# Cross attention, first pass: three moved steps on VectorE and GpSimd, and one weight split moved to the stage's start

## The chip, the cores and the metric

One Trainium2 chip, one of its cores. The metric is the device time of one launch in microseconds (us), median of the runs shown. A profile is one further execution recorded by the hardware profiler. Engines: PE (TensorE), DVE (VectorE), ACT (ScalarE), POOL (GpSimd), SP (the DMA queue's engine).

## The reference, cut to what matters

The reference is a decoder of two layers; the change lies in the cross attention of layer 1, here in short (b over 8 batches, 128 positions each, width 256):

```
ln   = layernorm(x)
q, k, v, qx = fp8(ln / in_scale_m) @ w_m          # four matrices m, fp8: clamp, bf16, round to e4m3
kx, vx = split(ctx @ w_kv_x)
q, k, qx, kx = layernorm over each head of 128
core = softmax(q k^T) v        (16 heads, 8 key/value heads)
xout = softmax(qx kx^T) vx
x   += fp8(concat(core, xout) / proj_smooth) @ wproj * scales
```

The sixteen-bit matmuls on float32 weights need each weight split beforehand into a high and a low part: high = fp16(w * s), low = w * s - high.

## The kernel before, in words

Every engine has its own instruction list, written out by hand, and the engines meet only at semaphores; an instruction that waits holds all that stands behind it on its engine. The attention is worked through in 32 groups g (NG = 32): groups 0 to 15 are the first pass (core), groups 16 to 31 the second (xout), and each batch b takes two groups of a pass, one for each half of the heads. Group g+1's projections are computed inside group g's iteration.

In an iteration, with the functions of `cross`:

- PE: `project` (L1982 first pass, L1974 for the second pass's keys and values), `score` (L1999) in two halves, `project_out` (L2028), `turn_p` (L2007), `mix` (L2015), `turn` (L1989). Ahead of the first projection of group 16 it waits for all weight splits (w.split at len(w.chunks) = 26).
- DVE: `biggest` twice (the maxima of the scores, L2121), `divide` (reciprocal L2128, product L2131) and `variance` of the next group (L2142) in turns, `normalise` three times (L2147), in odd groups `add_out` (L2173), `smoothed` twice (L2159), `clip` (L2166, then L1886 and L1887 of `fp8_vector`), and in some odd groups `quantise_x` of a later batch (L2114, L1886, L1887).
- ACT: `square` (L2270, L2275), `weigh` (the exponentials, L2299), `take_pT`, `take_v`, `take_x` in odd groups, `take_turned` (L2291), and in the even groups named in `later` one weight chunk by `split_scalar` (L1441, L1443).
- POOL: `root` three times for the next group (L2379 with the first, then the power L2383), `add_c` (L2368) and `round_c` (L2373), which round the clipped output of the group before to fp8 by an addition and a subtraction, `split_pool` (the low part, L1449) in the groups of `later`, `add_x` (L2357) in even groups and `round_x` (L2362, L2363) in odd ones, which do the same rounding for the input of a later batch.

The rounding of an input batch b passes from `take_x` (ACT) to `quantise_x` (DVE) to `add_x` (POOL) to `round_x` (POOL); `quantise_x(b)` also waits until `round_x(b-1)` is done. The rounding of the output passes from `clip` (DVE) to `add_c` and `round_c` (POOL, one iteration later).

There are 26 weight chunks of 1024 columns. Fifteen are split in the scan before (IN_LOOP), three behind it, one (chunk 18) at the start of the cross attention by `last_splits` and `last_low`, and chunks 19 to 25 in groups 2, 4, ... 14.

The order of POOL in the iteration, before:

```python
            if g + 1 < NG:
                root(g + 1, 0)
            if g:
                add_c(g - 1)
            if g + 1 < NG:
                root(g + 1, 1)
                root(g + 1, 2)
            if g:
                round_c(g - 1)
```

Of the kernel before, what the change touches and what calls it, by code (L numbers as in the profile page):

```python
# [13 lines left out]
B, S, D = 8, 128, 256  # L14
# [990 lines left out]
def scan(k):  # L1005
# [9 lines left out]
    c_rows = [A.take([N])]  # L1015
# [5 lines left out]
    unsplit = [A.take([k.proj.SPLIT]), k.XN[:, 0:k.proj.SPLIT // D, :].rearrange("p b d -> p (b d)")]  # L1021
# [163 lines left out]
        for i in range(w.IN_LOOP, w.IN_LOOP + 3):  # L1185
            w.split_scalar(act, i, (unsplit[0], c_rows[0])[i % 2])

    def last_splits(act):
        for i in range(w.IN_LOOP + 3, w.IN_LOOP + w.TAIL):
            w.split_scalar(act, i, (unsplit[0], c_rows[0])[i % 2])  # L1190

    k.last_splits = last_splits

    def tensor(pe):
        k.turn_tensor(pe, 3, 2)
# [77 lines left out]
        for i in range(w.IN_LOOP, w.IN_LOOP + 3):  # L1273
            w.split_pool(pool, i, (unsplit[0], c_rows[0])[i % 2])

    def last_low(pool):
        for i in range(w.IN_LOOP + 3, w.IN_LOOP + w.TAIL):
            w.split_pool(pool, i, (unsplit[0], c_rows[0])[i % 2])

    k.last_low = last_low  # L1280

# [3 lines left out]
class Projections:  # L1285
# [144 lines left out]
            last = pool.tensor_tensor(self.factor[:, c, :], self.factor[:, c, :], self.ranged[:, 0:4], ALU.mult)  # L1430
        last.then_inc(self.factors_ready, 1)

    IN_LOOP, TAIL = 15, 4

    def split_scalar(self, act, i, tmp, buffers=2):
        if i == 0:
# [358 lines left out]
def cross(k):  # L1795
# [299 lines left out]
    def vector(dve, link):  # L2095
# [101 lines left out]
        for g in range(NG):  # L2197
            nxt = g + 1 < NG
            biggest(g, 0)
            biggest(g, 1)  # L2200
            divide(g, 0)
            if nxt:
                variance(g + 1, 1)
            divide(g, 1)
            if nxt:
                variance(g + 1, 2)
            if g in beside:
                moe.scale(dve, beside.index(g))
            if g == 30:
                moe.take_comb(dve, 0, ps[:, 6, :])  # L2210
            if nxt:
                for j in range(3):
                    normalise(g + 1, j)
            if g % 2 == 1 and g > 2:
                add_out((g - 3) // 2)
                if g > 2 * B + 3 and g != 27:
                    stats_of((g - 3) // 2 - B - 1)
                if g == 25:
                    stats_of(3)
                    moe.var_vector(dve, 0)  # L2220
            smoothed(g, 0)
            smoothed(g, 1)
            clip(g)
            if g == 0:
                quantise_x(2)
            if g % 2 and (g + 5) // 2 < B:
                quantise_x((g + 5) // 2)
            if g == 24:
                moe.total_vector(dve, ps[:, 6, 0:moe.PIECES])
            if g == 25:  # L2230
                moe.normalise(dve, 0, 0)
            if g == 26:
                moe.take_logits(dve, link, 0, 0, ps[:, 6, :])
                moe.normalise(dve, 0, 1)
            if g == 27:
                moe.take_logits(dve, link, 0, 1, ps[:, 6, :])
            if g == 28:
                moe.route(dve, link, 0)
# [14 lines left out]
    def scalar(act, link):  # L2253
        k.norm_twice(act, 7, [0])

        def take_x(b):
            act.wait_ge(lnT_psum, b + 1)
            wait(act, xs_ready, b)
            for r, m in enumerate(ROW):
                for c in range(KC if b else 1):  # L2260
                    last = act.activation(xy[:, r, c * S:(c + 1) * S], ps[:, 6, c * P:(c + 1) * P], ACT.Identity,
                                          scale=x_w[:, c, m:m + 1], bias=x_b[:, c, m:m + 1])
            last.then_inc(xy_raw, 1)

        def square(g, j):
            act.wait_ge(proj_psum, 4 * g + j + 1)
            if j == 0:
                wait(act, rs_ready, 3 * (g - 1) + 1)
                for i in range(MAXB):
                    last = act.activation(sq_k[:, i, :], ps[:, j, i * HD:(i + 1) * HD], ACT.Square,  # L2270
                                          accum_out=var[:, j, i:i + 1])
                last.then_inc(sq_ready, 1)
            else:
                wait(act, var_done, 2 * (g - 1) + j)
                act.activation(sq[:, (j - 1) * MAXB:j * MAXB, 0:HD], ps[:, j, :].rearrange("p (h d) -> p h d", d=HD),  # L2275
                               ACT.Square).then_inc(sq_ready, 1)

        def take_v(g):
            act.wait_ge(proj_psum, 4 * g + 4)
            wait(act, mixed, 2 * (g - 1))  # L2280
            out = flat(val[g % 2])
            act.mul(out, ps[:, 3, :], vx_inv if place(g)[0] else v_inv).then_inc(v_ready, 1)

        def take_turned(g, j):
            act.wait_ge(turn_psum, 3 * g + j + 1)
            wait(act, scores, 2 * (g - 1))
            if j == 0:
                wt = norms[:, 6:8] if place(g)[0] else norms[:, 2:4]
            else:
                wt = norm_q[:, 2:4] if place(g)[0] else norm_q[:, 0:2]  # L2290
            act.activation(flat(turned[g % 2][:, MAXB * j:MAXB * j + MAXB, :]), ps[:, j, :], ACT.Identity,  # L2291
                           scale=wt[:, 0:1], bias=wt[:, 1:2]).then_inc(turn_ready, 1)

        def weigh(g, t):
            n = 2 * g + t
            act.wait_ge(mx_ready, n + 1)
            wait(act, rden_ready, n - 1)
            for i in range(MAXB):
                last = act.activation(ps[:, 4 + t, i * P:(i + 1) * P], ps[:, 4 + t, i * P:(i + 1) * P], ACT.Exp,  # L2299
                                      bias=mx[:, t, i:i + 1], accum_out=den[:, t, i:i + 1])  # L2300
            last.then_inc(probs, 1)

        def take_pT(g, t):
            n = 2 * g + t
            act.wait_ge(pT_psum, n + 1)
            wait(act, mixed, n - 1)
            act.copy(flat(pT[t]), ps[:, 4 + t, :]).then_inc(pT_ready, 1)  # L2307

        act.wait_ge(consts, 1)
        take_x(0)  # L2310
        k.last_splits(act)
        square(0, 0)
        k.norm_twice(act, 8, range(1, B))
        act.activation(k.warm[:, :], k.eps[:, 0:1], ACT.Exp)
        square(0, 1)
        square(0, 2)
        take_v(0)
        take_x(1)
        for j in range(3):
            take_turned(0, j)  # L2320
        for g in range(NG):
            nxt = g + 1 < NG
            if nxt:
                square(g + 1, 0)
            weigh(g, 0)
            if nxt:
                square(g + 1, 1)
            weigh(g, 1)
            if nxt:
                square(g + 1, 2)  # L2330
            take_pT(g, 0)
            if nxt:
                take_v(g + 1)
            if g in (26, 27):
                moe.take_turned(act, 0, g - 26, ps[:, 6, :])
            if g == 28:
                moe.exponential(act, 0)
            take_pT(g, 1)
            if g == 0:
                take_x(2)  # L2340
            if g % 2 and (g + 5) // 2 < B:
                take_x((g + 5) // 2)
            if g in later:
                w.split_scalar(act, w.IN_LOOP + w.TAIL + later.index(g), unsplit, 1)
            if g in squaring:
                moe.square_piece(act, squaring.index(g))
            if g in beside:
                moe.high_part(act, beside.index(g))
            if nxt:
                for j in range(3):  # L2350
                    take_turned(g + 1, j)

    def gpsimd(pool, link):
# [29 lines left out]
            pool.tensor_tensor(rs[:, j, :], var[:, j, :], minus_half[:, j, :], ALU.pow).then_inc(rs_ready, 1)  # L2383

        pool.wait_ge(xq_ready, 1)
        k.last_low(pool)
        pool.wait_ge(k.x_done, 4)
        pool.memset(moe.minus_half, -0.5)
        pool.memset(moe.one, 1.0)
        link(pool.memset(minus_half, -0.5))  # L2390
        pool.wait_ge(consts, 1)
        for j in range(3):
            root(0, j)
        for g in range(NG):
            if g == 0:
                add_x(1)
            if g + 1 < NG:
                root(g + 1, 0)
            if g:
                add_c(g - 1)  # L2400
            if g + 1 < NG:
                root(g + 1, 1)
                root(g + 1, 2)
            if g:
                round_c(g - 1)
            if g in later:
                pool.wait_ge(cy_ready, g + 1)
                w.split_pool(pool, w.IN_LOOP + w.TAIL + later.index(g), unsplit)
            if g % 2 == 0 and 0 < g and (g + 4) // 2 < B:
                add_x((g + 4) // 2)  # L2410
            if g == 0:
                round_x(1)
                add_x(2)
            if g % 2 and (g + 3) // 2 < B:
                round_x((g + 3) // 2)
            if g == 28:
                moe.total_pool(pool, link)
            if g == 25:
                moe.rstd_pool(pool, 0)
            if g in (26, 27):  # L2420
                moe.x_low(pool, 0, g - 26)
            if g in beside:
                moe.low_part(pool, beside.index(g))
# [325 lines left out]
```

## Time and profile before

| what | value |
|---|---|
| median of 3 runs | 1042.55 us (1041.51 to 1043.96) |
| the profiled execution, its own time | 1043.24 us |
| its span, first to last instruction | 1041.4 us |
| mean granted TensorE clock | 0.953 |
| busy share of the span | PE 86%, DVE 75%, ACT 64%, POOL 53% |
| cross attention, first maxima to the last | 407.8 to 803 us in the span |

All times in the rows are us from the start of the span; a timeline row gives start, length, engine, line, operation, output and inputs, and in brackets how long the engine had been idle and who released it.

### The profile page before, as it was taken

What the parts mean: (1) busy time and instruction counts of PE and PEld (TensorE: products, weight loads), DVE (VectorE), ACT (ScalarE), POOL (GpSimd) and SP (SyncE); (2) the same over time, 40 slices, a digit from 0 to 9 for tenths busy, and PEclk for the clock granted to TensorE, in tenths of its full rate; (3) what the DMA queues carried; (4) which work ended last, traced back from release to release, by engine and by line L of the source; (5) the groups of instructions that cost most, each with busy time, mean ns of one, the idle gap of its engine ahead of it and who ended that gap; (6) DMA issues with size and microseconds to landing.
All of it is one profiled execution on the core that took longest, in us unless ns stands there. A gap on an engine that the chain in (4) does not pass through costs nothing.

```text
span 1041.4 us, 16045 instructions
## 1 busy us (share of the span) xinstructions
PE 896.2 (86%) x5388; PEld 577.4 (55%) x5388; DVE 779.8 (75%) x1345; ACT 671.6 (64%) x1585; POOL 555.9 (53%) x422
## 2 busy tenths in 40 slices
PE   6898899567566657888889999999999998999998
PEld 3665543234122224666666767777777665556565
DVE  4578879887999987877777757778877766664454
ACT  2656479787766657988887867887766455433222
POOL 3312447261699964788888766677666443410000
PEclk9899899788799987999999999999999999999999
DMA  9832205001121100000000060230002421223221
GB/s 330 342 140 78 86 0 177 14 1 44 41 81 67 74 21 1 1 2 1 1 1 22 21 180 24 73 106 2 1 2 65 160 66 57 73 60 88 71 67 40
DMA packets 38725, 69.77 MB, mean 67 GB/s; under 512 B 5378, under 2 KB 25282, under 8 KB 37108
## 3 DMA queue, kind: packets, MB, share of 16 engines
q1 hardware_dynamic: 38644, 68.75, 20.0%
q8 instruction: 43, 0.70, 0.3%
q14 instruction: 38, 0.31, 0.1%
HBM read 67.56 MB, written 1.18 MB: 66 GB/s over the span
## 4 chain that ended last, share of the span: by engine, by line
PE 31%; DVE 24%; POOL 19%; issue 17%; ACT 6%; DMA 2%; SPq 0%; POOLq 0%; DVEq 0%; ACTq 0%
PE ps L2467 10%; DVE arena L1126 6%; PE ps L2496 5%; POOL arena L2383 5%; POOL arena L2368 5%; POOL arena L2373 4%; DVE ps L1122 4%; PE ps L451 2%; PE ps L491 1%; DMA wide<-in_w_down 1%; PE ps L727 1%; PE ps L729 1%; PE ps L728 1%; PE ps L484 1%; POOL arena L2357 1%
## 5 line engine op out<-in xcount | busy, mean ns | idle before, releaser
L2383 POOL TENSOR_TENSOR arena<-arena 128x4 f32<-128x4 f32 x96 | 99.1, 1034 | 47.2 <-DVE arena L2142 44.5
L2299 ACT ACTIVATE ps<-ps,arena 128x128 f32<-128x128 f32 x256 | 88.4, 354 | 33.6 <-DVE arena L2121 33.5
L2514 DVE TENSOR_TENSOR arena<-ps,arena 128x512 f32<-128x512 f32 (+1 forms) x56 | 38.7, 690 | 86.4 <-ACT ps L2507 86.4
L2467 PE MATMUL ps<-XT,wide 128*128 128x512 f16 (+1 forms) x384 | 92.4, 379 | 0.9 <-DVE arena L2533 0.9
L2507 ACT ACTIVATE ps<-ps,arena 128x512 f32<-128x512 f32 (+1 forms) x56 | 36.9, 659 | 82.1 <-PE ps L2467 82.1
L2291 ACT ACTIVATE arena<-ps,ones 128x512 f32<-128x512 f32 x96 | 68.3, 788 | 29.2 <-PE ps L1989 29.2
L2121 DVE TENSOR_REDUCE arena<-ps 128x4 f32<-128x512 f32 x64 | 43.5, 689 | 57.7 <-PE ps L1999 57.7
L1271 POOL TENSOR_TENSOR arena<-arena 128x1024 f32<-128x1024 f32 x31 | 72.9, 2354 | 21.1 <-DVE arena L1126 18.9
L2496 PE MATMUL ps<-wide,arena 128*128 128x256 f16 (+1 forms) x672 | 82.2, 272 | 0.1
L2496 PEld LDWEIGHTS ps<-wide,arena 128*128 128x128 f16 (+3 forms) x672 | 65.4, 98 | 19.9 <-issue 0.8
L1999 PEld LDWEIGHTS ps<-arena 128*128 128x128 f32 x512 | 68.6, 196 | 10.3 <-ACT arena L2291 1.2
L1126 DVE TENSOR_TENSOR_SCAN arena<-arena,ps 128x1024 f32<-128x1024 f32 x32 | 73.2, 2287 | 1.1
L1982 PE MATMUL ps<-wide,arena 128*128 128x512 f16 x256 | 66.3, 394 | 8.6 <-DVE arena L2108 5.5
L2028 PE MATMUL ps<-side,arena 128*128 128x256 f16 x512 | 71.9, 275 | 0.0
L2015 PE MATMUL ps<-arena 128*128 128x256 f32 x256 | 69.1, 395 | 0.9 <-ACT arena L2307 0.9
L1999 PE MATMUL ps<-arena 128*128 128x128 f32 x512 | 68.9, 279 | 0.7 <-ACT arena L2291 0.7
L2373 POOL TENSOR_TENSOR arena<-arena 128x1024 bf16<-128x1024 f32 x32 | 68.3, 2136 | 0.2
L2147 DVE TENSOR_TENSOR arena<-ps,arena 128x512 f32<-128x512 f32 x96 | 61.5, 683 | 7.5 <-POOL arena L2383 6.9
L1222 PE MATMUL ps<-arena,ident 128*128 128x512 f32 x128 | 61.7, 604 | 1.9 <-POOL arena L1271 1.6
L1179 ACT ACTIVATE arena<-arena 128x1016 f32<-128x1016 f32 x32 | 36.5, 1142 | 39.0 <-DVE arena L1126 39.0
L1405 POOL TENSOR_TENSOR wide<-wide,head_mean 128x1024 f32<-128x1024 f32 x12 | 22.7, 1896 | 71.0 <-DVE head_mean L1400 71.0
L2028 PEld LDWEIGHTS ps<-side,arena 128*128 128x128 bf16 x512 | 50.5, 99 | 16.1 <-issue 0.7
(341 smaller groups left out, 2371.1 us busy)
## 6 DMA issues: line engine op xcount, KB each, us to landing
arena<-scan_rows SPq DMA_DIRECT2D x16, 512.0 KB, 3.5
arena<-comb_rows SPq DMA_DIRECT2D x26, 256.0 KB, 3.2
side<-in_wproj SPq DMA_DIRECT2D x4, 1024.0 KB, 5.5
arena<-in_w_down SPq DMA_DIRECT2D x7, 512.0 KB, 3.8
wide<-in_w_down SPq DMA_DIRECT2D x1, 3584.0 KB, 15.9
side<-in_w_gate SPq DMA_DIRECT2D x1, 3520.0 KB, 19.4
side<-in_w_up SPq DMA_DIRECT2D x1, 3520.0 KB, 12.5
wide<-in_w_gate SPq DMA_DIRECT2D x2, 1728.0 KB, 12.2
```

The source lines that it names most:

```text
L1126: dve.tensor_tensor_scan(state[c], dA[c], product, 0.0, ALU.mult, ALU.add).then_inc(state_ready, 1)
L1271: pool.tensor_tensor(read[c], state[c], c_rows[n % 2], ALU.mult).then_inc((read0_ready, read1_ready)[c], 1)
L1982: last = pe.matmul(ps[:, bank, :], x[:, c * S:(c + 1) * S], rhs, start=(i == 0), stop=(i == len(steps) - 1))
L1999: last = pe.matmul(ps[:, 4 + t, i * P:(i + 1) * P], tt[:, MAXB + h, :], tt[:, h // 2, :], start=(i == 0), stop=True, skip_group_check=True)
L2015: last = pe.matmul(ps[:, 4 + t, 2 * i * P:(2 * i + 2) * P], val[g % 2][:, 2 * t + i, :], flat(pT[t][:, 2 * i:2 * i + 2, :]), start=(i == 0 ...
L2028: last = pe.matmul(ps[:, 7, 0:D], cq[g % 2][:, i, :], w.parts(k.side, ((2 * path + half) * QH + i) * D)[part][:, 0:D], start=(half == 0 an ...
L2291: act.activation(flat(turned[g % 2][:, MAXB * j:MAXB * j + MAXB, :]), ps[:, j, :], ACT.Identity, scale=wt[:, 0:1], bias=wt[:, 1:2]).then_i ...
L2299: last = act.activation(ps[:, 4 + t, i * P:(i + 1) * P], ps[:, 4 + t, i * P:(i + 1) * P], ACT.Exp, bias=mx[:, t, i:i + 1], accum_out=den[: ...
L2373: pool.tensor_tensor(flat(cq[g % 2]), flat(cs), flat(cm[g % 2]), ALU.subtract).then_inc(cq_ready, 1)
L2383: pool.tensor_tensor(rs[:, j, :], var[:, j, :], minus_half[:, j, :], ALU.pow).then_inc(rs_ready, 1)
L2467: last = pe.matmul(self.ps[0:m, 2 * up + n % 2, :], y[:, c, :], x[:, c, :], start=(t == 0), stop=(t == len(steps) - 1))
L2496: last = pe.matmul(self.out(b), x[0:m, b * S:(b + 1) * S], y[0:m, :], start=(j == 0 and b % 2 == 0 and t == 0), stop=(j == MC - 1 and t == 2),
```

## The change

Four edits, all in the cross attention.

1. DVE: `quantise_x` of batches 3 to 7 moves from the end of odd group g-1 to even group g, behind the two `biggest` and ahead of `divide`. Batches 1 and 2 stay where they were.
2. POOL: `round_x` in odd groups additionally waits for cy_ready, that is, for the end of `clip` of its own group.
3. POOL: in groups 1 to 15 `add_c` moves from between the first and the second `root` to behind the third.
4. One more chunk is split outside the loop: TAIL goes from 4 to 5. Chunk 19 is split at the start of the stage, by ACT behind chunk 18 into the spare buffer of the loop, by POOL between `root(0, 0)` and `root(0, 1)`. `later` shrinks to groups 2, 4, ... 12, and group 14 has no split.

```diff
-    def last_splits(act):
-        for i in range(w.IN_LOOP + 3, w.IN_LOOP + w.TAIL):
-            w.split_scalar(act, i, (unsplit[0], c_rows[0])[i % 2])
+    def last_split(act, i):
+        w.split_scalar(act, i, (unsplit[0], c_rows[0])[i % 2])
...
-    IN_LOOP, TAIL = 15, 4
+    IN_LOOP, TAIL = 15, 5
...
             biggest(g, 0)
             biggest(g, 1)
+            if g % 2 == 0 and g and (g + 4) // 2 < B:
+                quantise_x((g + 4) // 2)
             divide(g, 0)
...
             if g == 0:
                 quantise_x(2)
-            if g % 2 and (g + 5) // 2 < B:
-                quantise_x((g + 5) // 2)
...
         take_x(0)
-        k.last_splits(act)
+        k.last_split(act, w.IN_LOOP + 3)
+        w.split_scalar(act, w.IN_LOOP + 4, unsplit)
         square(0, 0)
...
-        k.last_low(pool)
+        k.last_low(pool, w.IN_LOOP + 3)
...
-        for j in range(3):
-            root(0, j)
+        root(0, 0)
+        w.split_pool(pool, w.IN_LOOP + 4, unsplit)
+        root(0, 1)
+        root(0, 2)
...
                 root(g + 1, 0)
-            if g:
+            if g >= 2 * B:
                 add_c(g - 1)
             if g + 1 < NG:
                 root(g + 1, 1)
                 root(g + 1, 2)
+            if 0 < g < 2 * B:
+                add_c(g - 1)
             if g:
                 round_c(g - 1)
...
             if g % 2 and (g + 3) // 2 < B:
+                pool.wait_ge(cy_ready, g + 1)
                 round_x((g + 3) // 2)
```

## Rows read from the trace of the kernel before

**Rows 1.** The page, busy time, share of the span and instructions.

```profile
PE 896.2 (86%) x5388; PEld 577.4 (55%) x5388; DVE 779.8 (75%) x1345; ACT 671.6 (64%) x1585; POOL 555.9 (53%) x422
```

**Rows 2.** Timeline: maxima that open groups 1, 2, 5, 6, 12, 15; PE: group 6's scores.

```profile
419.78 0.69 DVE L2121 TENSOR_REDUCE arena<-ps 128x4 f32<-128x512 f32 x1 [0.51 <-PE ps L1999]
...
432.94 1.28 DVE L2121 TENSOR_REDUCE arena<-ps 128x4 f32<-128x512 f32 x2
...
470.29 0.69 DVE L2121 TENSOR_REDUCE arena<-ps 128x4 f32<-128x512 f32 x1 [1.25 <-PE ps L1999]
...
481.13 1.05 PE L1999 MATMUL ps<-arena 128*128 128x128 f32 x8
...
485.07 1.28 DVE L2121 TENSOR_REDUCE arena<-ps 128x4 f32<-128x512 f32 x2
...
565.33 1.28 DVE L2121 TENSOR_REDUCE arena<-ps 128x4 f32<-128x512 f32 x2
...
604.85 0.69 DVE L2121 TENSOR_REDUCE arena<-ps 128x4 f32<-128x512 f32 x1 [5.96 <-PE ps L1999]
```

**Rows 3.** Timeline, GpSimd, from the split to the input's subtractions.

```profile
469.12 2.12 POOL L1449 TENSOR_TENSOR wide<-arena,wide 128x1024 f16<-128x1024 f32 x1 [1.29 <-DVE arena L1887]
471.20 2.12 POOL L2357 TENSOR_TENSOR arena<-arena 128x1024 f32<-128x1024 bf16 x1
...
474.55 2.13 POOL L2368 TENSOR_TENSOR arena<-arena 128x1024 f32<-128x1024 bf16 x1
476.63 2.00 POOL L2383 TENSOR_TENSOR arena<-arena 128x4 f32<-128x4 f32 x2
...
480.69 0.68 POOL L2362 TENSOR_TENSOR XT<-arena 128x256 bf16<-128x256 f32 x1
481.31 1.83 POOL L2363 TENSOR_TENSOR arena<-arena 128x768 bf16<-128x768 f32 x1
```

**Rows 4.** Timeline, three places where a rounding step of VectorE meets GpSimd.

```profile
432.36 1.06 POOL L2383 TENSOR_TENSOR arena<-arena 128x4 f32<-128x4 f32 x1
432.59 0.43 DVE L1887 TENSOR_SCALAR arena<-arena 128x1024 bf16<-128x1024 bf16 x1
...
481.69 1.75 DVE L1886 TENSOR_SCALAR arena<-XN 128x1024 uint16<-128x1024 uint16 x1
...
674.18 1.15 POOL L1681 TENSOR_TENSOR wide<-arena,wide 128x512 f16<-128x512 f32 x1
...
674.26 1.35 DVE L2166 TENSOR_SCALAR arena<-arena 128x1024 bf16<-128x1024 bf16 x1
```

**Rows 5.** Timeline, VectorE, steps of groups 5 and 6.

```profile
475.25 0.68 DVE L2142 TENSOR_REDUCE arena<-arena 128x4 f32<-128x516 f32 x1
...
478.67 0.69 DVE L2147 TENSOR_TENSOR arena<-ps,arena 128x512 f32<-128x512 f32 x1 [0.29 <-PE ps L1989]
...
480.98 0.67 DVE L2166 TENSOR_SCALAR XN<-XN 128x1024 bf16<-128x1024 bf16 x1
...
487.32 0.18 DVE L2128 RECIPROCAL arena<-arena 128x4 f32<-128x4 f32 x1 [0.97 <-ACT ps L2299]
...
488.14 0.68 DVE L2142 TENSOR_REDUCE arena<-arena 128x4 f32<-128x516 f32 x1
...
490.62 1.89 DVE L2147 TENSOR_TENSOR arena<-ps,arena 128x512 f32<-128x512 f32 x3
...
493.75 0.44 DVE L2166 TENSOR_SCALAR arena<-arena 128x1024 bf16<-128x1024 bf16 x1
```

**Rows 6.** Timeline, waits at the start of the stage.

```profile
391.99 0.28 ACT L2270 ACTIVATE arena<-ps 128x128 bf16<-128x128 f32 x1 [3.64 <-PE ps L1982]
...
398.78 1.08 POOL L2383 TENSOR_TENSOR arena<-arena 128x4 f32<-128x4 f32 x1 [4.16 <-DVE arena L2142]
```

**Rows 7.** Timeline, TensorE, the keys of group 16 behind the loop's last split.

```profile
601.14 1.96 PE L1974 MATMUL ps<-wide,CT 128*128 128x512 f16 x6 [3.07 <-POOL side L1449]
```

**Rows 8.** Windows by stage: us, then each engine's busy time (instructions), then PEclk.

```profile
516.00:521.00 5.00, 4.76 (x20) 3.78 (x21) 3.50 (x7) 3.48 (x5) 3.11 (x2) 0.66 0.01 2
```

More of the change, by code:

```diff
@@ L1186, in scalar @@
             w.split_scalar(act, i, (unsplit[0], c_rows[0])[i % 2])
-    def last_splits(act):
-        for i in range(w.IN_LOOP + 3, w.IN_LOOP + w.TAIL):
-            w.split_scalar(act, i, (unsplit[0], c_rows[0])[i % 2])
-    k.last_splits = last_splits
+    def last_split(act, i):
+        w.split_scalar(act, i, (unsplit[0], c_rows[0])[i % 2])
+    k.last_split = last_split
     def tensor(pe):
@@ L1274, in gpsimd, with last_low @@
             w.split_pool(pool, i, (unsplit[0], c_rows[0])[i % 2])
-    def last_low(pool):
-        for i in range(w.IN_LOOP + 3, w.IN_LOOP + w.TAIL):
-            w.split_pool(pool, i, (unsplit[0], c_rows[0])[i % 2])
+    def last_low(pool, i):
+        w.split_pool(pool, i, (unsplit[0], c_rows[0])[i % 2])
     k.last_low = last_low
```

## The prediction

> **What bounds the kernel now.** I read the page first. TensorE is busy for 86% of the span and GpSimd for 53% [rows 1], but the change lies in the cross attention's first pass alone, so what counts is which chain sets the pace there. A timeline of VectorE's maxima gives that pace, since each group opens with one [rows 2]. From group 2 to group 6 pass 52.13 us, 26.07 for a pair (an odd and an even group). The pair is uneven: from group 5 to group 6 it takes 14.78, so the even group takes 11.3. From group 6 to group 12, three pairs take 80.26, 26.75 each, and from 12 to 15, three groups take 39.52.
>
> The reader is to see in [rows 2] that an odd group's maxima wait for TensorE's scores (1.25 us idle), while an even group's two come back to back without a bracket: there the scores were ready and VectorE was late. What made it late stands in [rows 4]: L1886, 0.43 us elsewhere in the same view, took 1.75 us beside the input's subtraction L2363 [rows 3], which ran to 483.14. It got through at 483.44 less 0.43, that is 483.01, 0.1 ahead of the recorded end. The same is seen at 674.26, where L2166 took 1.35 beside a split. So a clipping step and a long GpSimd operation exclude each other. Behind the clipping came the input's rounding, three steps more, and only then the maxima at 485.07, while the scores had been there from 482.18 on [rows 2].
>
> The second bound is the last weight split [rows 7]. TensorE stands idle 3.07 us ahead of group 16's keys until the split of group 14 is done, just ahead of 601.14, and VectorE is idle 5.96 us ahead of group 15's maxima [rows 2].
>
> **The change part by part.**
>
> *The split in the gap.* ACT waits 3.64 us at 391.99 and GpSimd 4.16 at 398.78 [rows 6]. ACT's two steps (a scaling and a cast) end before 397.3 in any case and within the 3.64 if they take the 2.12 that GpSimd's half takes [rows 3]; GpSimd's 2.12 goes into its 4.16. I cost both at nothing; uncovered they would cost 2.1 each, late next being the first squares and the second root. No DMA moves. What is won in group 14 is both halves of its split, and TensorE's wait with it.
>
> *Odd groups 3 to 11.* The new order of GpSimd, counted from the end C of the even group's clipping, by the pitches of [rows 3]: start 0.1; split 2.08; input's addition and first root 3.35; two roots 1.97 (done at 7.5); output's addition 2.08 (to 9.6); output's subtraction 2.1 (to 11.7). The variances do not hold it: the second is done 5.64 after the maxima [rows 2, 5]. VectorE's third normalisation follows the third root at 7.54, and the clipping asks 2.31 later (478.67 to 480.98) [rows 5], at 9.85. By then the output's subtraction has begun at 9.6: the clipping is caught until 11.6, then needs 1.35 (three steps of 0.43 at a pitch of 0.46). So the next maxima come at **12.95** in place of 14.78. The input's rounding no longer stands ahead of them, and its subtractions, now waiting, catch nothing. Behind that new wait on GpSimd stand the next group's first root and all later sums, and VectorE's moved rounding waits for it. TensorE and ACT do not decide: group 6's scores ended at 482.18, 11.9 behind group 5's maxima [rows 2].
>
> *Even groups 2 to 10.* From the end of the odd clipping: input's subtractions 0.1 + 0.62 + about 1.7 (1.83 in [rows 3], with a clipping step slipped in) = 2.4. The moved rounding waits for them, then takes 1.35: 3.75. It stands ahead of both divisions. Reciprocal to variance is 0.82 (487.32 to 488.14) [rows 5], and 0.60 to the next reciprocal, which finds its exponentials done: the second variance starts at 3.75 + 0.82 + 0.60 + 0.82 = 5.99 and ends at 6.67. Third root 7.7, addition 9.8, subtraction 11.9. The third normalisation at 7.75 and 1.93 from there to the clipping (490.62 to 493.75, less two normalisations of 0.60) [rows 5] give 9.68, within 0.1 of the boundary between the two sums. Slipping in ahead of the subtraction it ends at 13.0, caught at 13.1. So **13.0** in place of 11.3: the even group pays for its rounding.
>
> The pair thus takes 25.95. Five pairs, groups 2 to 11: before 52.13 + 80.26 = 132.39, after 129.75, **-2.6**. Half of it is group 8's: at 516 to 521 the granted clock was 0.66 [rows 8], part of the time at the 1.2 GHz level, which then lay on TensorE's path and now hides behind GpSimd.
>
> *Group 1.* It has no split ahead. Second variance at 5.64, third root 6.7, addition 8.8, subtraction 10.9, clipping done by 12.1, so maxima of group 2 at 419.78 + 12.0 = 431.8 against 432.94 [rows 2]: **-1.15**.
>
> *Groups 12 to 14.* Without the input's steps the variance at 5.64 paces them as in group 1, 12.2 each, 36.6 against 39.52: **-2.9**. In it is what the last split gives, most of the 5.96 idle ahead of group 15's maxima, less what the new order costs, since the sums now lie on the clipping in these groups too.
>
> *From group 15 on* the order is the old one; nothing of the experts' stage is touched, and what the cross attention gives is passed on.
>
> Sum: -1.15 - 2.6 - 2.9 = -6.7. The profiled execution took 1043.24 (its span 1041.4 and 1.8 around it), so 1036.5; it lies 0.7 above the median of the runs, against which the sum gives **1035.8**.
>
> *A rule that speaks against it.* In [rows 4] GpSimd's power L2383 runs from 432.36 for 1.06 us, and VectorE's L1887 beside it keeps its 0.43: a power, which moves four elements, does not hold VectorE up. The Trainium skill (SBUF — State Buffer, Who interferes with whom) says that a VectorE operation in a two-port mode and a GpSimd operation exclude each other for the whole instruction. By that rule the first root, which now runs beside the moved rounding, would cost it the power's length; the sum would be that of the second rival below. The trace agrees with the rule for the long operations and not for this short one.
>
> **The rivals.**
>
> 1. *The sums do not catch the clipping.* Then an odd group takes the 11.9 of its scores and an even one 11.3 and at most the rounding's 1.35: the pair 24.55, 1.4 less, 7 over five pairs: 1028.8. For it: no row shows L2368 or L2373 itself beside a clipping step. Against: L2363 and L1681 have the same form and catch it. 9%.
> 2. *The first pass gives nothing.* Each half is longer by 0.3 to 0.5 (the root's power holding the rounding for 1.0 in five even groups makes +5, hence 1040.8; the clipping's steps caught apart make about +3), and only the last split's gain stays: 1038.5 to 1040.8, at the middle 1039. For it: my sums agree with the old pair to within 0.12. 22%.
> 3. *Slower: the clipping is caught by both sums.* Place: odd groups 3 to 11, where the addition might start late (a root held by its variance) and the clipping meet addition and subtraction, 2.1 more, 15.0 in place of 12.95, with the even groups' 1.7 loss staying. Five times 2.1 is +10.5: 1046. It decides from 1.35 more a pair. Against it: the roots' inputs are ready at 5.64, two ahead of need, and the subtraction is the last operation before GpSimd waits. 6%.
> 4. *The change does not do what it says*: TensorE's wait ahead of group 16 is replaced by another (the weights' or the squares' transfer) and the pairs balance: 1042.5. Against it: [rows 7] names the split alone. 4%.
>
> **How the numbers follow.** The forecast, GpSimd pacing every group of the first pass, has 59%; its own range is 13 groups by 0.25, 1032.5 to 1039. The range for all cases leaves out rival 1, rival 3 and rival 4, 19%, and takes in the second: 1030 to 1040.8. A measurement of this kernel tells 0.2%, 2.1 us, from no change (its three runs spread by 2.5). Faster: forecast, rivals 1 and 2, less a little at the edge: 0.90; same 0.04; slower 0.06.
>
> **What would show it.** Right: maxima of odd groups 12.9 to 13.1 after the even ones and the other way round, instead of 14.8 and 11.3; no idle bracket on TensorE's scores at those maxima; a clipping step of 1 to 2.5 us in every odd group, now beside L2373 and not L2363; GpSimd without idle time in odd groups; ACT's gap at 392 shrunk to about 1.4, nothing after it later; TensorE not idle ahead of L1974; groups 12 to 14 near 12.2. Wrong: odd groups near 12, clipping steps all at 0.43 (rival 1); moved rounding steps of over 1 us (rival 2); two long clipping steps in one group (rival 3); maxima of group 15 still over 4 us idle (rival 4).

## The result, and the profile after

The changed kernel takes 1036.6 us (median of 11 runs, 1033.1 to 1040.5), the kernel before 1045.3 in the same rounds (11 runs, 1041.5 to 1047.9): ratio 0.9922, 95% interval 0.9904 to 0.994, about 8 us faster. One run of a kernel tried below (no wait) took 1116.9 us at a mean granted clock of 0.822, against 0.953 to 0.964 in its other runs, and stands in no ratio. The profiled executions have spans of 1041.4 and 1035.0. A reader who compares those two alone gets 6.4, since group 1's maxima came 1.43 later in the second. Of that, 1.07 was there when the stage's first squares began (391.99 and 393.06).

The page of the changed kernel, busy time by engine, answers to [rows 1]:

```profile
PE 887.2 (86%) x5372; PEld 571.7 (55%) x5388; DVE 796.9 (77%) x1345; ACT 671.9 (65%) x1585; POOL 554.2 (54%) x422
```

No engine gained or lost work. TensorE shows 9 us less, with 16 matmul records fewer, all of them ahead of the stage. VectorE is 17 us more busy in a span 6 shorter, with as many instructions as before; the busy time is steps that sit and wait inside their own records. The average says nothing of where. The pace does. Timeline of VectorE in the changed kernel, the maxima that open groups 1, 2, 5, 6, 12 and 15, which answer to [rows 2]:

```profile
421.21 0.69 DVE L2119 TENSOR_REDUCE arena<-ps 128x4 f32<-128x512 f32 x1 [0.50 <-PE ps L1997]
...
433.08 0.69 DVE L2119 TENSOR_REDUCE arena<-ps 128x4 f32<-128x512 f32 x1
...
471.63 0.68 DVE L2119 TENSOR_REDUCE arena<-ps 128x4 f32<-128x512 f32 x1
...
484.65 1.29 DVE L2119 TENSOR_REDUCE arena<-ps 128x4 f32<-128x512 f32 x2
...
562.58 1.41 DVE L2119 TENSOR_REDUCE arena<-ps 128x4 f32<-128x512 f32 x2
...
598.79 0.68 DVE L2119 TENSOR_REDUCE arena<-ps 128x4 f32<-128x512 f32 x1
```

Odd group 5 takes 13.02 in place of 14.78. The bracket ahead of group 5's first maxima is gone: the first half of the scores is ready and waits for VectorE in every group from 2 to 9 (the second maxima of group 5 still wait 0.59 us for theirs). Ahead of group 15 the 5.96 us of idle time are gone too. What holds VectorE is seen beside GpSimd; first VectorE, then GpSimd, groups 5 and 6 of the changed kernel (they answer to [rows 3] to [rows 5]):

```profile
481.56 2.25 DVE L2164 TENSOR_SCALAR XN<-XN 128x1024 bf16<-128x1024 bf16 x1
483.85 0.43 DVE L1884 TENSOR_SCALAR arena<-XN 128x1024 uint16<-128x1024 uint16 x1
...
487.19 0.43 DVE L2112 TENSOR_SCALAR arena<-arena 128x1024 bf16<-128x1024 bf16 x1 [1.24 <-POOL arena L2362]
...
494.40 0.43 DVE L2164 TENSOR_SCALAR arena<-arena 128x1024 bf16<-128x1024 bf16 x1
494.86 2.24 DVE L1884 TENSOR_SCALAR arena<-arena 128x1024 uint16<-128x1024 uint16 x1
```

```profile
479.19 2.13 POOL L2367 TENSOR_TENSOR arena<-arena 128x1024 f32<-128x1024 bf16 x1
481.40 2.14 POOL L2372 TENSOR_TENSOR arena<-arena 128x1024 bf16<-128x1024 f32 x1
...
487.32 1.25 POOL L2382 TENSOR_TENSOR arena<-arena 128x4 f32<-128x4 f32 x1
490.02 1.01 POOL L2382 TENSOR_TENSOR arena<-arena 128x4 f32<-128x4 f32 x1 [1.45 <-DVE arena L2140]
...
492.41 2.14 POOL L2367 TENSOR_TENSOR arena<-XN,arena 128x1024 f32<-128x1024 bf16 x1
494.62 2.19 POOL L2372 TENSOR_TENSOR arena<-arena 128x1024 bf16<-128x1024 f32 x1
```

The clipping's first step asks at 481.56, 0.16 behind the start of the output's subtraction at 481.40, and takes 2.25 instead of 0.43; in the even group the first step slips in and the second takes 2.24. The catch of 1.75 in [rows 4] was not removed but handed to another operation of GpSimd, and a second one was made in the even group.

The start of the stage and its last wait, ACT and TensorE of the changed kernel (they answer to [rows 6] and [rows 7]):

```profile
393.06 0.28 ACT L2268 ACTIVATE arena<-ps 128x128 bf16<-128x128 f32 x1 [1.51 <-PE ps L1980]
```

```profile
596.36 1.46 PE L1972 MATMUL ps<-wide,CT 128*128 128x512 f16 x6
```

ACT's gap shrank from 3.64 to 1.51, so the split is covered: from the first squares to the first maxima pass 16.08 us here and 15.84 in the kernel before, and 15.62 in three of the kernels below that have the moved split too. TensorE goes into group 16's keys without a bracket, at 1.46 for the six matmuls in place of 1.96.

What the pace alone does not show is TensorE's granted clock. Windows from one group's maxima to the next give it behind the busy times (1.00 is the 2.4 GHz level, 0.50 the 1.2 GHz level); groups 8 and 10, the kernel before, then the changed one:

```profile
511.14:524.09 12.95, 10.39 (x62) 7.94 (x61) 8.69 (x18) 10.49 (x33) 7.35 (x5) 0.87 0.00 1
538.88:551.79 12.91, 10.27 (x60) 7.79 (x59) 8.68 (x18) 10.49 (x33) 7.36 (x5) 0.87 0.01 2
```

```profile
510.48:523.31 12.83, 10.94 (x76) 8.11 (x75) 11.36 (x21) 10.78 (x34) 9.99 (x8) 1.00 0.01 2
536.32:550.34 14.02, 12.02 (x71) 8.82 (x70) 10.34 (x21) 10.60 (x33) 10.56 (x9) 0.88 0.01 2
```

Before, two even groups ran in part at the lower level and took 12.9 in place of 11.27; in the changed kernel it is one, and it took 14.02 in place of 12.83, after which group 11 took 12.24 in place of the 13.01 of the other odd groups. This decides how the pairs' gain is to be read. With every group at the length that it has at full clock (an estimate from the rows of the neighbouring groups; group 11 of the changed kernel at 13.01), groups 2 to 11 add up to 129.05 before and 129.08 after. The odd groups' gain is paid for by the even ones, and the 2.9 us that the two profiled executions differ by in these groups is the lower clock: it cost 3.3 us before and 0.4 after.

### The profile page after: what moved, and what is told of

Its sections match the earlier page's. It is cut to its first block, busy times and chain, and to the rows that moved or that the text cites. A ratio compares the mean times of both kernels' runs of the same rounds, so it can differ in the third digit from the quotient of the medians.

```text
span 1035.0 us, 16028 instructions
## 1 busy us (share of the span) xinstructions
PE 887.2 (86%) x5372; PEld 571.7 (55%) x5388; DVE 796.9 (77%) x1345; ACT 671.9 (65%) x1585; POOL 554.2 (54%) x422
## 4 chain that ended last, share of the span: by engine, by line
PE 30%; DVE 24%; POOL 19%; issue 17%; ACT 8%; DMA 2%; SPq 0%; POOLq 0%; DVEq 0%; ACTq 0%
PE ps L2471 10%; DVE arena L1126 6%; PE ps L2500 5%; POOL arena L2382 5%; POOL arena L2367 5%; POOL arena L2372 5%; DVE ps L1122 4%; PE ps L451 2%; PE ps L491 1%; DMA wide<-in_w_down 1%; PE ps L484 1%; PE ps L727 1%; PE ps L729 1%; PE ps L728 1%; ACT ps L2297 1%
## 6 DMA issues: line engine op xcount, KB each, us to landing
wide<-in_w_down SPq DMA_DIRECT2D x1, 3584.0 KB, 16.2
wide<-in_w_gate SPq DMA_DIRECT2D x2, 1728.0 KB, 12.2
```

## The experiments

The tables give the time from one group's maxima to the next, from the profiled execution of each kernel (differences of rows like those above). The sum runs from group 1's maxima to group 16's. The column on the clock names the groups 1 to 14 in which the mean granted clock was below 1.00, and what it was. Ratios are to the kernel before, with their intervals.

| kernel | edits in it | group 1 | odd 3 to 9 | even 2 to 10 | 12, 13, 14 | sum | lower clock in | ratio |
|---|---|---|---|---|---|---|---|---|
| before | none | 13.16 | 14.8 | 11.27; 12.9 in 8, 10 | 12.31, 11.20, 16.01 | 197.42 | 8, 10 (0.87), 14 (0.91) | 1 |
| changed | 1, 2, 3, 4 | 11.87 | 13.0 | 12.7 to 12.8; 14.0 in 10 | 12.30, 12.16, 11.75 | 189.93 | 10 (0.88) | 0.9922 (0.9904 to 0.994) |
| split alone | 4 | 13.16 | 14.8 | 11.29; 12.8, 12.6, 14.3 in 6, 8, 10 | 12.32, 11.21, 11.72 | 194.98 | 6 (0.87), 8 (0.86), 10 (0.76) | 0.9953 (0.9937 to 0.9969) |
| no split | 1, 2, 3 | 11.88 | 13.0; 12.3 in 7 | 12.8; 13.95 in 6 | 12.32, 12.15, 18.59 | 197.30 | 6 (0.88), 14 (0.85) | 0.9989 (0.9978 to 1.0001) |
| no wait | 1, 3, 4 | 12.12 | 14.0 to 14.7 | 11.8 to 13.0 | 12.31, 12.16, 11.76 | 194.75 | 6, 8, 10 (0.87) | 0.9951 (0.9926 to 0.9976) |
| addition between roots | 1, 2, 4 | 11.89 | 12.0 to 12.1 | 12.35; 13.75 in 2 | 12.31, 11.21, 11.71 | 182.45 | none | 0.9844 (0.9823 to 0.9864) |
| addition mixed | 1, 2, 3 in odd groups to 11, 4 | 11.88 | 12.15 | 12.35; 12.23 in 2 | 12.32, 11.21, 11.72 | 181.56 | none | 0.9846 (0.9826 to 0.9865) |
| rounding back | 2, 3, 4 | 15.57 | 16.2 to 16.8 | 12.2 to 12.8 | 12.32, 12.16, 11.76 | 205.30 | 2, 4, 6, 8, 10 (0.86 to 0.87) | 1.0073 (1.0048 to 1.0099) |
| rounding back, addition between | 2, 4 | 14.03 | 15.8 | 11.3 to 13.4 | 12.31, 11.21, 11.70 | 197.77 | 4 (0.87), 6, 8 (0.86), 10 (0.74) | 1.0009 (0.9993 to 1.0025) |
| no wait, addition between | 1, 4 | 11.89 | 13.5 | 12.7 to 13.8 | 12.32, 11.20, 11.71 | 194.20 | 6, 8, 10 (0.88) | 0.9974 (0.9961 to 0.9986) |

Theory A, which the experiments were to try: the gain is two separate ones, TensorE's wait of group 14 and GpSimd's order in the pairs, and what sets the pairs is GpSimd's chain with the mutual exclusion of its long operations and VectorE's clipping steps. Rival B: the split made nearly all of it. Each kernel was profiled once. That the lower clock falls where the pairs are long is seen in the column above (none where a pair takes under 25 us, five groups where it takes 29); what makes it fall was not tried. Over all runs the mean granted clock of the whole program goes the same way: its median is 0.950 and 0.951 in the two kernels with the rounding back, 0.955 in the kernel before (in the same rounds), 0.958 in the changed one and 0.960 in the two fastest.

### The split alone, and all but the split

The kernel before with edit 4; then the changed kernel without it:

```diff
-    IN_LOOP, TAIL = 15, 5
+    IN_LOOP, TAIL = 15, 4
...
-        w.split_scalar(act, w.IN_LOOP + 4, unsplit)
...
-        w.split_pool(pool, w.IN_LOOP + 4, unsplit)
```

> The kernel before with edit 4 alone (chunk 19 split at the stage's start, none in group 14), the orders of VectorE and GpSimd as before. Theory A (two separate gains: group 14's wait, and GpSimd's new order in the pairs): pairs stay at 26.07, group 1 at 13.2, groups 12 to 15 fall from 39.5 to about 35, so -4.4 us against the kernel before. Rival B (the split made nearly all of it; the pairs' gain was a lower granted clock that happened to fall away in group 8): -6 to -8 us, the lower clock in group 8 gone here too.

> The changed kernel without edit 4: group 14 splits its chunk again. Theory A: pairs at 25.84 as in the changed kernel, group 1 at 11.9, group 14's maxima to group 15's back at 16 to 16.5, TensorE idle some 3 us ahead of group 16's keys; -3.3 us against the kernel before, +4.4 against the changed one. Rival B: within 1 us of the kernel before.

Measured: 0.9953 and 0.9989. The split alone gives 4.9 us, near A's 4.4; group 14 falls from 16.01 to 11.72 and the other groups stay, save where the granted clock was lower (groups 6, 8 and 10 are 1.3 us and more over 11.29 each). Rival B expected 6 to 8 us, and the lower clock gone from group 8; the lower clock was there, and the interval, 3.2 to 6.6 us, reaches the low end of its range only.

The second run is a miss for A: edits 1 to 3 alone give 1.2 us, not 3.3, and the interval (2.3 faster to 0.1 slower) does not tell it from nothing. By its size it is nearer to B, which expected it within 1 us of the kernel before. So the split is needed for nearly all of the gain, but not for B's reason. Its pairs are as expected, 12.8 and 13.0, and so is group 1. Group 14 is not: 18.59, not 16 to 16.5. GpSimd, VectorE and TensorE there:

```profile
595.17 2.19 POOL L2371 TENSOR_TENSOR arena<-arena 128x1024 bf16<-128x1024 f32 x1
595.42 2.23 DVE L1884 TENSOR_SCALAR arena<-arena 128x1024 uint16<-128x1024 uint16 x1
...
598.18 2.12 POOL L1447 TENSOR_TENSOR side<-arena,side 128x1024 f16<-128x1024 f32 x1 [0.82 <-DVE arena L1885]
600.36 2.74 PE L1972 MATMUL ps<-wide,CT 128*128 128x512 f16 x6 [4.86 <-POOL side L1447]
```

The clipping is caught there too, the split stands behind the clipping, and TensorE behind the split: 4.86 us idle in place of 3.07. By the time its six matmuls start the granted clock is at 0.50, and stays there until 606; in the kernel before it fell to 0.50 at 602, one microsecond into them. They took 2.74, 1.96 in the kernel before and 1.46 at full clock. So the split's wait has two parts: in the kernel before group 14's 4.29 us over the split alone are 2.97 until the keys start and 1.32 behind that start, at the lower clock. With the new order they are 4.78 and 2.06, together 6.84. The two gains are not separate: the new order adds 2.6 us to group 14 and 0.95 to group 13, against 1.3 gained in group 1 and the pairs' 2.9. By the ratios, moving the split is worth 7 us with the new order (0.9989 to 0.9922) against 5 with the old one, a difference that their intervals alone would not show.

### Without the wait ahead of the input's subtractions

```diff
             if g % 2 and (g + 3) // 2 < B:
-                pool.wait_ge(cy_ready, g + 1)
                 round_x((g + 3) // 2)
```

> The changed kernel without edit 2: the input's subtractions on GpSimd no longer wait for the clipping. Theory A (a clipping step and a long GpSimd operation exclude each other): in odd groups the three clipping steps are caught one after another, by the output's subtraction and by both of the input's, so odd groups take about 15.0 in place of 13.0, even groups about 11.9 in place of 12.8 since the moved rounding no longer waits; the pair 26.9, +1.1, over five pairs +5 us against the changed kernel. Rival C (the wait is neutral, the subtractions merely start later): even groups 11.9, odd ones 13.0, -4 us against the changed kernel.

Measured 0.9951, 3 us over the changed kernel by ratio (the two intervals overlap), 4.8 in the sum of groups. The three clipping steps of group 5 in this kernel:

```profile
482.06 2.24 DVE L2164 TENSOR_SCALAR XN<-XN 128x1024 bf16<-128x1024 bf16 x1
484.34 0.78 DVE L1884 TENSOR_SCALAR arena<-XN 128x1024 uint16<-128x1024 uint16 x1
485.15 1.75 DVE L1885 TENSOR_SCALAR arena<-arena 128x1024 bf16<-128x1024 bf16 x1
```

Each is caught by another operation of GpSimd (the output's subtraction, then the input's two), as expected; group 5 takes 14.68 against the 15.0 forecast. Rival C, which expected 4 us less than the changed kernel, is out. The wait pays: the pair of groups 3 and 4, at full clock in both kernels, takes 26.44 without it and 25.84 with it. Groups 6, 8 and 10 ran at 0.87 here, so that a part of the 4.8 is the lower clock.

### The addition between the roots again

```diff
-            if g >= 2 * B:
+            if g:
                 add_c(g - 1)
             if g + 1 < NG:
                 root(g + 1, 1)
                 root(g + 1, 2)
-            if 0 < g < 2 * B:
-                add_c(g - 1)
```

> The changed kernel without edit 3: the output's addition is again between the first and the second root. Theory A: the addition fills GpSimd's 1.45 us of idle ahead of the second root in even groups, and the subtraction is done when the clipping comes: even groups fall from 12.8 to the 12.2 that the scores set, odd ones grow from 13.0 to 13.3 because the third normalisation waits for its root; the pair 25.5, and groups 13 and 14 about 0.5 to 0.9 shorter: -2 to -3 us against the changed kernel. Rival D (the third root's lateness is what counts, as the 1.16 us bracket ahead of the second normalisation in the kernel before suggests): every odd group longer by 1.2, +5 us.

Measured 0.9844: 16 us under the kernel before and some 8 under the changed one. The direction is A's, rival D is out, but A expected 2 to 3. VectorE and GpSimd in one odd group:

```profile
479.93 0.69 DVE L2145 TENSOR_TENSOR arena<-ps,arena 128x512 f32<-128x512 f32 x1 [1.25 <-POOL arena L2382]
...
483.22 0.43 DVE L2164 TENSOR_SCALAR XN<-XN 128x1024 bf16<-128x1024 bf16 x1
483.68 0.43 DVE L1884 TENSOR_SCALAR arena<-XN 128x1024 uint16<-128x1024 uint16 x1
484.14 0.43 DVE L1885 TENSOR_SCALAR arena<-arena 128x1024 bf16<-128x1024 bf16 x1
484.49 0.68 DVE L2119 TENSOR_REDUCE arena<-ps 128x4 f32<-128x512 f32 x1
```

```profile
471.35 2.13 POOL L1447 TENSOR_TENSOR wide<-arena,wide 128x1024 f16<-128x1024 f32 x1 [1.28 <-DVE arena L1885]
...
480.84 2.14 POOL L2372 TENSOR_TENSOR arena<-arena 128x1024 bf16<-128x1024 f32 x1
484.65 0.67 POOL L2361 TENSOR_TENSOR XT<-arena 128x256 bf16<-128x256 f32 x1 [1.67 <-DVE arena L1885]
```

The stall of the second normalisation is back (1.25; 1.16 in the kernel before, 0.29 in the changed one), and it costs nothing: the subtraction is done at 482.98 and all three clipping steps take 0.43. From the clipping's end ahead of the group (471.28, when GpSimd starts) to its end at 484.57 it is 13.3, as expected. What the expectation left out is the head start. The even group's clipping is no longer caught, ends 1.1 us ahead of the next maxima, and GpSimd sets off that much earlier; so counted from the maxima the odd group takes 12.07. The pair falls to 24.4, and group 13 takes 11.21 as in the kernel before. No group ran at the lower clock, which is a part of the gain over the other kernels, if a small one over the changed kernel (0.4 of 7.5 us in the sum).

Group 2 took 13.75 at full clock: its moved rounding was caught by the output's addition (436.71 for 2.01 beside an addition at 436.32). What sets the other even groups at 12.35 stands in TensorE's rows, the second of the transposes that wait for VectorE's product, in group 6 of the kernel before and then of this one:

```profile
490.16 0.65 PE L2007 MATMUL ps<-ident,arena 128*128 128x128 f32 x4 [0.79 <-DVE arena L2131]
```

```profile
490.65 0.66 PE L2005 MATMUL ps<-ident,arena 128*128 128x128 f32 x4 [0.32 <-DVE arena L2129]
```

It starts 5.09 behind the maxima (485.07) before and 6.16 behind them (484.49) here, and in both the next maxima come 6.2 later, with no idle time of TensorE between. So the 1.1 us over the 11.27 of the kernel before is the rounding that now stands ahead of the divisions.

### The addition moved in odd groups alone

```diff
-            if g >= 2 * B:
+            if g and (g % 2 == 0 or g > 11):
                 add_c(g - 1)
...
-            if 0 < g < 2 * B:
+            if g % 2 and g <= 11:
                 add_c(g - 1)
```

> The changed kernel with edit 3 kept in odd groups up to 11 alone; in even groups and from 12 on the addition is again between the first and the second root. Theory A (what costs is the output's subtraction lying on the clipping, above all in even groups): even groups 12.35 as with edit 3 undone everywhere, clipping steps of odd groups caught again but ended at 11.9 to 12.0 behind the maxima, since GpSimd starts 1.1 us ahead of them: within 1 us of the kernel with edit 3 undone, some 7 us under the changed kernel. Rival E (a caught clipping step costs its full length wherever it is): odd groups 13.0, +5 us against the kernel with edit 3 undone.

Measured 0.9846, no difference from the kernel with the addition always between the roots. The odd group's first clipping step is caught again:

```profile
477.69 2.23 DVE L2164 TENSOR_SCALAR XN<-XN 128x1024 bf16<-128x1024 bf16 x1
...
480.76 0.68 DVE L2119 TENSOR_REDUCE arena<-ps 128x4 f32<-128x512 f32 x1
```

yet the maxima come 12.15 behind the last ones. Rival E is out: a caught step costs only what it ends later than the scores. The same catch goes with 13.0 us a group in the changed kernel, where GpSimd had no head start.

### The input's rounding back in its old place

The changed kernel without edit 1, and the same with the addition between the roots:

```diff
-            if g % 2 == 0 and g and (g + 4) // 2 < B:
-                quantise_x((g + 4) // 2)
...
+            if g % 2 and (g + 5) // 2 < B:
+                quantise_x((g + 5) // 2)
```

> The changed kernel without edit 1: the input's rounding on VectorE is again at the end of the odd group, while the subtractions it waits for still stand behind the clipping. Theory A: the maxima of even groups wait for the clipping, 2.4 of subtractions and 1.35 of rounding: odd groups 16.7, even groups 12.1; +3 a pair, +15 us against the changed kernel. Rival F (the rounding fits in VectorE's waits wherever it stands): +0 to +3 us.

> Edits 2 and 4 alone: as the kernel with edit 3 undone, and the input's rounding back at the end of odd groups. Theory A: odd groups 12.05 + 2.4 + 1.35 = 15.7, even groups 11.3; the pair 27.0 against 24.4: +13 us against the kernel with edit 3 undone, and slower than that by edit 4 alone. Rival F: +0 to +3 us.

Measured 1.0073 and 1.0009, 16 and 17 us over the kernels with the rounding moved (15 and 13 expected), with more groups at the lower clock than in any other kernel. VectorE in the first of them, odd group:

```profile
492.50 0.43 DVE L2112 TENSOR_SCALAR arena<-arena 128x1024 bf16<-128x1024 bf16 x1 [2.45 <-POOL arena L2362]
...
493.77 1.28 DVE L2119 TENSOR_REDUCE arena<-ps 128x4 f32<-128x512 f32 x2
```

The rounding waits 2.45 us for the subtractions, and the maxima stand behind it. Rival F (0 to 3 us) is out. With edit 2 in, edit 1 is needed.

### No wait, and the addition between the roots

Edits 1 and 4 alone.

> Edits 1 and 4 alone: as the kernel with edit 3 undone, and GpSimd's subtractions of the input again unwaiting. Theory A: in odd groups the clipping is caught by the subtractions (one step of 0.7, one of 2.1), odd groups 13.75; even groups 11.3 since the rounding does not wait and ends before the exponentials; the pair 25.05 against 24.4: +3 us against the kernel with edit 3 undone. Rival C (the wait is neutral): odd 12.05, even 11.3, -5 us.

Measured 0.9974: 14 us over the kernel with edit 2, not 3. Odd groups 13.54 are near the 13.75 expected; even ones are not 11.3 but 12.7 in group 4 at full clock, and 13.7 to 13.8 in groups 6, 8 and 10, which ran at 0.88. About 3 of the 14 us thus go with the lower clock. VectorE and GpSimd at the head of an even group:

```profile
488.48 2.12 DVE L2112 TENSOR_SCALAR arena<-arena 128x1024 bf16<-128x1024 bf16 x1
```

```profile
488.20 2.12 POOL L2367 TENSOR_TENSOR arena<-XN,arena 128x1024 f32<-128x1024 bf16 x1
```

Here the moved rounding is the one that is caught, by the output's addition, which GpSimd reaches early because nothing holds it. The expectation had looked for catches at the clipping alone. The rounding took 1.7 to 2.1 in all five even groups. The wait of edit 2 does more than save the clipping: it keeps GpSimd's next sum off the rounding, save in group 2 of the kernel with edit 3 undone.

## Why the prediction was right, point by point

- **Odd groups**: 12.95 predicted, 13.0 measured in groups 3 to 9. **Even groups**: 13.0 predicted, 12.8 measured; which of the two steps would be caught was left open, and it was the second, the first slipping in. Five pairs: -2.6 predicted, 132.39 to 129.50, -2.9 measured. The lengths are right, but what they are worth is luck in part: at full clock a pair goes from 26.07 to 25.84, and group 11, which had no rounding to lose, from 13.54 to 13.01, while even group 2 adds 1.4. That comes to nothing over the ten groups; the 2.9 is the lower clock, as worked out above.
- **Group 1**: -1.15 predicted, 13.16 to 11.87, -1.3 measured.
- **Groups 12 to 14**: -2.9 predicted, 39.52 to 36.21, -3.3 measured. Groups 12 and 13 took 12.3 and 12.2 as summed; group 14 took 11.75, not 12.2: the maxima that end it came 0.1 behind the end of the scores (598.70). Of what the last split gives, 1.3 is the lower clock that followed TensorE's idle time.
- **The split's cover**: costed at nothing; both gaps held it.
- **Group 8's lower clock** was to hide behind GpSimd, and to be half of the pairs' term. Group 8 took 12.83, but it ran at full clock, so it shows no hiding. Group 10, whose lower clock before (12.91) the prediction did not name, had it again and took 14.02, 1.2 unhidden, of which group 11 gave 0.8 back. The lower clock moved from group to group over the kernels tried, so that the pairs' term rests on where it fell in the one execution of each that was profiled.
- **The sum**: -6.7 predicted; the groups give -7.5, what follows group 16's maxima another -0.3, and the ratio 8 us. The terms were each low by 0.1 to 0.4, all the same way. That the measured 1036.6 lies within 1 us of the 1035.8 forecast is luck too: over all rounds the kernel before took 1045.3 and not the 1042.55 that was subtracted from.
- **Rival 1** was right about what uncaught clipping steps would be worth in the pairs (24.55 for a pair; 24.4 measured once edit 3 was undone), and wrong that this change would give it. **Rival 2's** mechanism did not happen, though its size, the first pass giving nothing, is what the profiled pairs give at full clock. Beside the moved rounding the first root's power (487.32) took 1.25 in place of 1.02, and the rounding's steps at 487.19, 487.65 and 488.11 kept their 0.43. By the rule of the Trainium skill (SBUF — State Buffer, Who interferes with whom) that the later of the two waits for the other's whole instruction, the second step would have waited until the power's end at 488.57. The trace agrees with the rule for the long operations and has the power as the one that gave way here, by 0.23. **Rivals 3 and 4** did not happen.
- What the prediction did not see is that edit 3 costs 8 us. It is in the working all the same: both of its caught steps came from edit 3's order, and it summed them without asking what the old order would give beside the other edits.
- That the last split costs more with the new order (6.84 us in group 14, against 4.29) was not in the terms either; they had been taken as independent.

The best version tried is the changed kernel with edit 3 undone: 1029.6 us against 1044.9 in the same rounds, ratio 0.9844 (0.9823 to 0.9864). Its even groups are held at 12.35 by the moved rounding ahead of the divisions; a third place for it was not tried. Nor was any kernel tried with the clock as its aim.

## What to carry to other kernels

When two engines exclude each other, an operation is placed by what it will meet, not by who waits for it: moving the additions ended a 1.2 us stall of VectorE and put a 2.1 us operation onto a 1.35 us one, twice a pair. Sum both engines side by side from the same origin, with the head start that one change gives the next, and try each edit of a bundle undone: beside the split, edits 1 and 2 lose 2 and 6 us when the other is left out, and gain 11 when both are in, of which edit 3 gave back 8. Read the granted clock of each group beside its length before crediting a gain to an order: here it makes up the pairs' whole difference between the two profiled executions.

## What was not expected of the hardware

- A waiting step of VectorE gets in between two GpSimd instructions that follow each other without a gap: in the changed kernel the addition started at 492.41 for 2.14, the clipping's first step ran at 494.40 for 0.43, and the subtraction started at 494.62, for 2.19 rather than 2.14. It started no later behind the addition (2.21) than in the odd group, where nothing got in between (479.19 to 481.40).
- Busy time of VectorE rose by 17 us with no work added (779.8 to 796.9), 16 of it in the three steps that round to fp8, whose records grew (the clipping's first step on odd groups from 8.6 to 20.1 in all); a busy share can therefore not be read as work.
- After an idle time of 4.86 us TensorE's six matmuls L1972 took 2.74 us, at a granted clock of 0.50; after 3.07 they (L1974) took 1.96, at full clock until 602 and at 0.50 behind it; with no idle time ahead and at full clock 1.46. In the kernel before the lower level lasted from 602 to about 605.4, well after TensorE was busy again.
- The lower clock needs no such gap: in group 8 of the kernel before it set in at 516.7, behind waits of TensorE of 1.77 and 0.79 us, while group 6 ran at full clock behind waits of 1.74 and 0.79. What tells the two apart is not shown.
